# Last head of an expert-mixing attention layer: half of its output columns by slots instead of by dense products

## The chip, the cores and the metric

One core of one Trainium2 chip. The metric is the device time of the kernel in microseconds. TensorE (PE), VectorE (DVE), ScalarE (ACT), GpSimd (POOL) and SyncE (SP) run their own instruction streams side by side and wait for each other only through semaphores. SP issues most transfers; POOL issues the indirect ones.

## The reference, cut to what matters

`x` is 384 tokens by 1024. A graph attention layer is added to it first (the change does not touch it). Then comes a layer with 8 attention heads, each with 8 experts for its values and 8 experts for its output:

```python
gate_o = _get_sel_gate(x, sel_o_w, rs)        # per token and head: 8 gates, all but the best 2 are zero
ctx = jnp.einsum('bhqk,bhkp->bqhp', att, v)   # per token and head: 128 values
weighted = ctx[:, :, :, None, :] * gate_o[..., None]
out = jnp.einsum('bshep,hepd->bsd', weighted, o_w.reshape(H, E, P, D))
x = x + out
```

So a head's output is a sum over 8 experts, and for each token six of the eight terms are zero.

## The kernel before, in words

The kernel has two ways to compute a head's output.

**Dense.** All 8 experts for all tokens. The context is multiplied by each gate (`gate_context(e)` on DVE), turned on PE (`gated_turns(e)`), and split into a rounded part (`gc_hi_of`, ACT) and a rest (`gc_lo_of`, DVE). Weights come in units of 128 x 1024 through a ring of 3 buffers: SP loads (`load_unit`), ACT rounds (`hi_ring`), POOL or DVE makes the rest (`lo_of`). A product is three matmuls (`three`). One dense unit is 2 experts x 3 token tiles x 3 matmuls of 512 columns, for half of the output columns; 8 units (d0 to d7) cover the 1024 columns.

**By slots.** Each token with one of its two experts is a row, 768 rows a head. They are sorted by expert into 1024 slots, in lanes of 32 rows that share an expert. For head h: DVE scales the context rows (`gate_rows_of(h)`, 6 instructions); POOL scatters them to slots in DRAM (`scatter_rows`, 6 indirect transfers); SP loads the slots back (`load_slots`); PE turns them (`slot_turns`); ACT and DVE copy them out (`gcT_of`). DVE makes one-hot tables (`make_hots`), PE finds the output row of each slot from them (`rows_of_slots`), DVE stores it (`find_rows`). Then 8 rounds (`output_round(h, r)`) on PE, each 4 lanes x 2 column halves; of a round's four lanes two read their expert's weights where they were loaded, the other two a copy (`copy_out`, even ones on DVE, odd ones on ACT). After each round ACT and DVE bring the result from its banks to a stage (`y_out`), and POOL adds the stage's rows into `sums_scratch` in DRAM (`add_rows`, an indirect transfer that accumulates). The two rows of one token go to two different parts of `sums_scratch` (768 x 1024 in all), the first of which also holds x.

Heads 0 to 6 go by slots, head 7 is dense. The loop for h = 1 to 7 computes head h's queries, keys and values and attends, and in between does the slots of head h - 1. So in its last turn (h = 7) PE does the rounds of head 6: rounds 0 to 3, `f_attend(7)`, round 4, `context_turns(7)`, rounds 5 and 6, `gated_turns(0)`, round 7. After the loop the 8 dense units follow on PE.

The order on every engine is written out by hand. On POOL the loop's end is `lo_of` d0 and d1 and the eight `add_rows(6, i)`, then `lo_of` d3 to d7. `add_rows(h, 0)` waits until all eight adds of the head before have landed (`y_landed`), since an accumulating transfer must not meet another one on the same row. On SP, `load_sums` waits for all adds of head 6, then loads the two parts of the sums (3 tiles of 128 x 1024 each). DVE adds the parts (`add_sums`) and then the dense result of each column half (`add_out`, `add_out_tile`); SP stores six pieces of 128 x 512.

Of the kernel before, what the change touches and what calls it, by code (L numbers as in the profile page):

```python
# [14 lines left out]
P = 128  # L15
N = 384
NT = N // P
D = 1024
# [28 lines left out]
def ring_order():  # L47

    yield "v", 0, 0
    yield "router",  # L50
    yield "v", 0, 1
    for h in range(FH):
        yield "q", h
        yield "k", h
        for i in range(0 if h else 2, 8):
            yield "v", h, i
    for i in range(8):
        yield "d", i
# [36 lines left out]
OF_LAST = ((7, 5, 6), (0, 3, 4))  # L95
# [32 lines left out]
def landed(h):  # L128

    return 16 * h  # L130

# [33 lines left out]
def gnn_switch_kernel(nc, x_in, units, biases, bo, edge_type_weights, route_scale, edge_cols, src_row, dst_row, out):  # L165
# [5 lines left out]
    with ctx:  # L171
# [50 lines left out]
        gated = scratch[:, 4224:4992].rearrange("p (b n) -> p b n", b=2)  # L222
# [47 lines left out]
        row_of = edge_words[:, 0:(FH - 1) * SLOTS].rearrange("p (h i) -> p h i", h=FH - 1)  # L270
# [46 lines left out]
        gated_T, sums_landed, sums_added = sem("gated_T"), [sem(f"sums_landed{t}") for t in range(NT)], sem("sums_added")  # L317
        fq_hi_done, fq_lo_done, fk_hi_done, fk_lo_done = (sem("fq_hi_done"), sem("fq_lo_done"), sem("fk_hi_done"),
# [19 lines left out]
        def turned(g):  # L338
            return bank[(7, 6)[g]][:]
# [24 lines left out]
        def _(sp):  # L364
# [76 lines left out]
            for h in range(1, FH):  # L441
# [9 lines left out]
                load_unit(*(("q", h + 1) if h < FH - 1 else ("d", 0)))  # L451
                load_unit(*(("k", h + 1) if h < FH - 1 else ("d", 1)))
                load_unit(*(("v", h + 1, 0) if h < FH - 1 else ("d", 2)))
            def load_sums(n):
                if n == 0:
                    for b in range(STAGES):
                        sp.wait_ge(y_landed[b], landed(FH - 1))
                dst = x[:, n, :] if n < NT else y_rows[n - NT]
                sp.dma_start(dst, sums_dram[n * P:(n + 1) * P, :]).then_inc(sums_landed[n % NT], 16)
# [17 lines left out]
        def _(pool):  # L477
# [110 lines left out]

            lo_of("q", 0)
# [7 lines left out]
            for h in range(1, FH):  # L597
# [25 lines left out]
        def _(act):  # L623
# [209 lines left out]

            def q_hi(h):
# [5 lines left out]
            def gcT_of(h):  # L840
                act.wait_ge(slots_T, 2 * h + 1)
                act.activation(by_halves(gcT[:].rearrange("p a n -> p (a n)"), 0),
                               turned(0).rearrange("p (b n) -> p b n", n=GD), ACT.Copy).then_inc(gcT_act, 1)
# [29 lines left out]
            for h in range(1, FH):  # L873
# [19 lines left out]
                hi_ring(*(("q", h + 1) if h < FH - 1 else ("d", 0)))  # L893
                copy_out(h - 1, 9)
                hi_ring(*(("k", h + 1) if h < FH - 1 else ("d", 1)))
                hi_ring(*(("v", h + 1, 0) if h < FH - 1 else ("d", 2)))
# [14 lines left out]
            for e in range(1, FE):  # L911
                gc_hi_of(e)
                if e % 2:
                    if e > 1:
                        hi_ring("d", (e + 3) // 2)
            hi_ring("d", 6)
            hi_ring("d", 7)

# [3 lines left out]
        def _(dve):  # L922
# [524 lines left out]

            def gcT_of(h):
                dve.wait_ge(slots_T, 2 * h + 2)
                dve.tensor_copy(by_halves(gcT[:].rearrange("p a n -> p (a n)"), 1),  # L1450
                                turned(1).rearrange("p (b n) -> p b n", n=GD)).then_inc(gcT_dve, 1)
# [22 lines left out]

            def add_out(f, need, banks):
                dve.wait_ge(unit_used, need)
                for t in range(NT):
                    add_out_tile(f, t, banks)
# [59 lines left out]
            def gate_context(e):  # L1538
                if e == 0:
                    dve.wait_ge(context_T, FH)  # L1540
                    dve.wait_ge(gated_rows_landed, 16 * 6 * (FH - 1))
                if e >= 2:
                    dve.wait_ge(gated_T, e - 1)
                c = (GROUPS - 1) * FE + e
                dve.tensor_tensor(gated[:, e % 2, :].rearrange("p (t d) -> p t d", t=NT),
                                  bank[turned_bank(FH - 1)][:, 0:N].rearrange("p (t d) -> p t d", t=NT),
# [6 lines left out]
            def add_sums(t):  # L1553
                dve.wait_ge(sums_landed[t], 32)
                dve.tensor_tensor(x[:, t, :], x[:, t, :], y_rows[t], ALU.add).then_inc(sums_added, 1)

            gate_context(0)
            y_out(FH - 2, SLOTS - 3)
            gate_context(1)
            lo_of("d", 2)  # L1560
            y_out(FH - 2, SLOTS - 2)
            gc_lo_of(0)
            y_out(FH - 2, SLOTS - 1)
            gate_context(2)
            for e in range(1, FE):
                gc_lo_of(e)
                if e + 2 < FE:
                    gate_context(e + 2)
            for t in range(NT):
                add_sums(t)  # L1570
# [508 lines left out]
```

## Time and profile before

| what | value |
|---|---|
| median of 3 runs | 824.06 us (823.68 to 826.8) |
| profiled execution, its own time | 826.44 us |
| its span, first to last instruction | 824.4 us |
| granted TensorE clock over the span | 0.998 |
| busy: PE, DVE, POOL, ACT | 812.7, 489.0, 461.0, 376.4 us |

The span is what the trace shows. The profiled execution's own time is 2.04 us more than its span, and 2.38 us more than the median. Times in rows below are microseconds from the span's start; a matmul's duration overlaps the next one, so its pace is read from the starts.

### The profile page before, as it was taken

The numbers are of one execution on the slowest core, as the hardware profiler recorded it, in microseconds if no ns is written. First come the engines' busy times: TensorE is split into PE (matmuls) and PEld (weight loads), VectorE is DVE, ScalarE is ACT, GpSimd is POOL, SyncE is SP. The second block draws the span as 40 slices with busy tenths as digits, with TensorE's granted clock in tenths as the row PEclk, the third lists the DMA queues.
The fourth block names the chain that finished last, engine by engine and source line by source line (L and its number), as shares of the span: only waits on it lengthen the run. The fifth ranks groups of instructions, "written<-read, shape, count | busy, mean of one in ns | idle before, by whom it ended". The sixth has DMA issues, their size and how long they took to land.

```text
span 824.4 us, 14155 instructions
## 1 busy us (share of the span) xinstructions
PE 812.7 (99%) x5016; PEld 650.6 (79%) x5016; DVE 489.0 (59%) x1112; ACT 376.4 (46%) x615; POOL 461.0 (56%) x296
## 2 busy tenths in 40 slices
PE   8999999999999999999999999999999999999998
PEld 7999998888888778898578578578578588588476
DVE  7999973444444155998554554655655545645645
ACT  5333335555665343334624634634634534535531
POOL 4577875343334434547664665565674665664652
PEclk9999999999999999999999999999999999999999
DMA  8666663442222328643598597597597597697684
GB/s 295 185 194 178 201 191 107 144 136 81 97 76 78 103 77 323 213 129 134 122 245 304 119 266 273 125 264 269 132 271 258 131 264 261 140 257 262 147 217 172
DMA packets 66177, 153.38 MB, mean 186 GB/s; under 512 B 9392, under 2 KB 22320, under 8 KB 66128
## 3 DMA queue, kind: packets, MB, share of 16 engines
q1 hardware_dynamic: 51472, 120.73, 42.7%
q0 software_dynamic: 10944, 24.82, 16.5%
q10 hardware_dynamic: 3712, 7.18, 3.2%
q8 instruction: 30, 0.49, 0.3%
q14 instruction: 19, 0.16, 0.1%
HBM read 122.06 MB, written 37.97 MB: 194 GB/s over the span
## 4 chain that ended last, share of the span: by engine, by line
PE 83%; POOL 4%; issue 4%; DMA 3%; DVE 3%; ACT 1%; SPq 0%; ACTq 0%; DVEq 0%; POOLq 0%
PE bank L1586 22%; PE bank L1588 21%; PE bank L1587 21%; PE bank L1917 12%; POOL mask_scratch L501 3%; PE bank L1640 2%; PE bank L1729 2%; PE bank L1633 2%; PE bank L1701 2%; DVE scratch L1004 1%; DMA w_raw<-in_units 1%; DMA mask_scratch<-scratch,cell 1%; POOL w_lo L497 1%; DMA mask<-mask_scratch 0%; ACT scratch L725 0%
## 5 line engine op out<-in xcount | busy, mean ns | idle before, releaser
L557 POOL TENSOR_TENSOR w_lo<-w_raw,w_hi 128x1024 fp32r<-128x1024 f32 x67 | 164.4, 2456 | 140.3 <-ACT w_hi L812 132.2
L1586 PE MATMUL bank<-w_hi,hT_hi 128*128 128x512 f32 x480 | 190.1, 396 | 1.9 <-POOL w_lo L548 1.2
L1588 PE MATMUL bank<-w_hi,hT_lo 128*128 128x512 f32 x480 | 187.5, 391 | 0.0
L1587 PE MATMUL bank<-w_lo,hT_hi 128*128 128x512 f32 x480 | 187.5, 391 | 0.0
L497 POOL TENSOR_TENSOR w_lo<-w_raw,w_hi 128x1024 fp32r<-128x1024 f32 x39 | 94.7, 2431 | 103.7 <-ACT w_hi L640 83.5
L812 ACT ACTIVATE w_hi<-w_raw 128x1024 fp32r<-128x1024 f32 x84 | 88.7, 1056 | 127.0 <-PE bank L1588 98.9
L1586 PE MATMUL bank<-hT_hi,w_hi 128*128 128x384 f32 x320 | 108.2, 338 | 1.2 <-POOL w_lo L497 1.2
L1586 PEld LDWEIGHTS bank<-w_hi,hT_hi 128*128 128x128 f32 x480 | 90.6, 189 | 21.7 <-POOL w_lo L548 1.7
L1588 PE MATMUL bank<-hT_hi,w_lo 128*128 128x384 f32 x320 | 107.1, 335 | 0.0
L1587 PE MATMUL bank<-hT_lo,w_hi 128*128 128x384 f32 x320 | 107.1, 335 | 0.0
L1588 PEld LDWEIGHTS bank<-w_hi,hT_lo 128*128 128x128 f32 x480 | 90.1, 188 | 19.1
L1587 PEld LDWEIGHTS bank<-w_lo,hT_hi 128*128 128x128 f32 x480 | 90.2, 188 | 17.4
L1917 PE MATMUL bank<-late,gcT 128*32 128x512 f32 (+1 forms) x868 | 100.6, 595 | 0.0
L1917 PEld LDWEIGHTS bank<-late,gcT 128*32 128x32 f32 x868 | 26.7, 109 | 57.2 <-issue 55.0
L501 POOL DMA_INDIRECT mask_scratch<-scratch,cell x48 | 56.9, 1185 | 23.8 <-issue 12.9
L1586 PE MATMUL bank<-large,w_hi 128*128 128x384 f32 x192 | 66.5, 346 | 0.0
L1586 PEld LDWEIGHTS bank<-hT_hi,w_hi 128*128 128x128 f32 x320 | 60.2, 188 | 7.3 <-issue 5.0
L1587 PE MATMUL bank<-large,w_hi 128*128 128x384 f32 x192 | 65.0, 339 | 0.0
L1588 PE MATMUL bank<-large,w_lo 128*128 128x384 f32 x192 | 64.9, 338 | 0.0
L1414 DVE COPY late<-late 128x1024 f32 x56 | 60.6, 1112 | 6.3 <-issue 5.3
L1587 PEld LDWEIGHTS bank<-hT_lo,w_hi 128*128 128x128 f32 x320 | 60.1, 188 | 0.0
L1588 PEld LDWEIGHTS bank<-hT_hi,w_lo 128*128 128x128 f32 x320 | 60.1, 188 | 0.0
(228 smaller groups left out, 1279.6 us busy)
## 6 DMA issues: line engine op xcount, KB each, us to landing
w_raw<-in_units SPq DMA_DIRECT2D x145, 512.0 KB, 3.9
late<-in_units SPq DMA_DIRECT2D x56, 512.0 KB, 7.7
scratch<-slots_scratch SPq DMA_DIRECT2D x7, 512.0 KB, 7.3
scratch<-in_src_row ACTq DMA_DIRECT2D x8, 384.0 KB, 4.3
scratch<-in_dst_row ACTq DMA_DIRECT2D x8, 384.0 KB, 6.3
sums_scratch<-zeros SPq DMA_DIRECT2D x1, 1536.0 KB, 8.3
sums_scratch<-x SPq DMA_DIRECT2D x1, 1536.0 KB, 11.3
x<-sums_scratch SPq DMA_DIRECT2D x3, 512.0 KB, 4.8
```

What stands on the lines that cost most here:

```text
L497: pool.tensor_tensor(w_lo[:, s, :], w_raw[:, s, :], w_hi[:, s, :].bitcast(fp32), ALU.subtract).then_inc(lo_ready[s], 1)
L501: pool.indirect_dma_start(out=mask_dram, out_offset=bass.IndirectOffsetOnAxis(ap=cells, axis=0), in_=values, in_offset=None, bounds_check= ...
L557: pool.tensor_tensor(w_lo[:, s, :], w_raw[:, s, :], w_hi[:, s, :].bitcast(fp32), ALU.subtract).then_inc(lo_ready[s], 1)
L812: act.activation(w_hi[:, s, :], w_raw[:, s, :], ACT.Copy).then_inc(hi_ready, 1)
L1414: dve.tensor_copy(copied[:, m % COPY_BUFS, :], late[:, bass.ds(copy_value[m // 2], D)]).then_inc(copied_dve, 1)
L1586: pe.matmul(dst, a_hi, b_hi, start=first, stop=False)
L1587: pe.matmul(dst, a_hi, b_lo, start=False, stop=False)
L1588: return pe.matmul(dst, a_lo, b_hi, start=False, stop=last)
L1633: return pe.transpose(dst, src, ident[:])
L1640: last = pe.transpose(banks[g][:, i * GD:(i + 1) * GD], block[rows, :], ident[rows, rows])
L1701: last = pe.matmul(bank[NT * head + t][:, 0:N], a[p, tok], b[p, :], start=n == 0, stop=n == 2)
L1917: last = pe.matmul(bank[YF[r % 2][f]][lane * LANE:(lane + 1) * LANE, :], gcT[:, r // 4, c:c + LANE], weights, start=True, stop=True)
```

## The change

Head 7's output columns 512 to 1023 stay dense (units d4 to d7, now the only ones in the ring). Its columns 0 to 511 go by slots, in eight half rounds (`last_round`) with one bank each. Their weights (units d0 to d3) are loaded straight to `o_raw`. For head 7 there are now also `gate_rows_of`, six `scatter_rows` (put between `add_rows(6, 3)` and `add_rows(6, 4)`), `load_slots`, `slot_turns`, `make_hots`, `rows_of_slots`, `find_last_rows`, 15 copies of 512 columns, eight `last_y_out` and eight `last_add_rows`, whose rows are 512 wide. The sums are loaded in two lots: columns 512 to 1023 once head 6's adds have landed, columns 0 to 511 once head 7's have. Round 3 of head 6 is moved behind `f_attend(7)`, round 4 behind `context_turns(7)`, and ACT's `context_of(7)` ahead of `y_out(6, 3)`. Whole for SP and POOL; for the others the orders are written on fewer lines:

```diff
-OF_LAST = ((7, 5, 6), (0, 3, 4))
+OF_LAST = (7, 3, 4)
+LAST = FH - 1
...
-gated = scratch[:, 4224:4992].rearrange("p (b n) -> p b n", b=2)
+gated = [copied[:, b, HALF:HALF + N] for b in (8, 9)]
...
 # sync: after the loads of the last turn (d4, d5, d6)
-for i in range(3, 7):
-    load_unit("d", i)
-for n in range(NT):
-    load_sums(n)
 load_unit("d", 7)
-for n in range(NT, 2 * NT):
-    load_sums(n)
-for f in range(2):
-    for t in range(NT):
-        sp.wait_ge(out_added, 2 * NT + NT * f + t + 1)
-        sp.dma_start(out_tiles[:, t, f * HALF:(f + 1) * HALF],
-                     x[:, t, f * HALF:(f + 1) * HALF]).then_inc(out_stored, 16)
+sp.wait_ge(y_done, SLOTS * LAST)
+for i in range(4):
+    sp.dma_start(out_part(o_raw, 2 * i),
+                 units[PLACE["d", i]].rearrange("p (k n) -> p k n", k=2)).then_inc(o_landed, 16)
+load_slots(LAST)
+def load_sums(f, landings):
+    cols = slice(f * HALF, (f + 1) * HALF)
+    for n in range(2 * NT):
+        t = n % NT
+        dst = x[:, t, :] if n < NT else stage(t)
+        sp.dma_start(dst[:, cols], sums_dram[n * P:(n + 1) * P, cols]).then_inc(landings[t], 16)
+for b in range(STAGES):
+    sp.wait_ge(y_landed[b], landed(LAST))
+load_sums(1, sums_landed)
+for b in range(STAGES):
+    sp.wait_ge(y_landed[b], landed(FH))
+load_sums(0, last_landed)
+for t in range(NT):
+    sp.wait_ge(out_added, 2 * NT + t + 1)
+    sp.dma_start(out_tiles[:, t, HALF:D], x[:, t, HALF:D]).then_inc(out_stored, 16)
...
 # gpsimd
+def last_add_rows(i):
+    if i % 2:
+        pool.wait_ge(y_dve, last_dve_rows(i + 1))
+    else:
+        pool.wait_ge(y_act, last_act_rows(i + 1))
+    if i == 0:
+        pool.wait_ge(rows_known, FH)
+        for b in range(STAGES):
+            pool.wait_ge(y_landed[b], landed(LAST))
+    pool.indirect_dma_start(out=sums_dram.rearrange("r (f n) -> (r f) n", f=2),
+                            out_offset=bass.IndirectOffsetOnAxis(ap=row_of[:, LAST, i:i + 1], axis=0),
+                            in_=stage(i)[:, 0:HALF], in_offset=None, bounds_check=4 * N - 1,
+                            oob_is_err=False, compute_op=ALU.add).then_inc(y_landed[i], 16)
...
-        lo_of("d", 0)
-        lo_of("d", 1)
+        lo_of("d", 4)
+        lo_of("d", 5)
     for i in range(SLOTS):
+        if h == LAST and i == 4:
+            for k in range(2):
+                for t in range(NT):
+                    scatter_rows(LAST, k, t)
         add_rows(h - 1, i)
-for i in range(3, 8):
-    lo_of("d", i)
+lo_of("d", 7)
+for i in range(SLOTS):
+    last_add_rows(i)
...
 # scalar (last_copy_out and last_y_out: as on vector)
+            if h == LAST and i == 3:
+                context_of(h)
             y_out(h - 1, i, 0)
-            if i == 3:
+            if h < LAST and i == 3:
                 context_of(h)
...
+gc_hi_of(1), (2), (3); hi_ring("d", 7); copy_experts(LAST)
+last_copy_out(1), (3); gc_hi_of(4); gcT_of(LAST); gc_hi_of(5); last_copy_out(5), (7)
+last_y_out(0); last_copy_out(9); last_y_out(2); last_copy_out(11); last_y_out(4)
+last_copy_out(13); last_y_out(6); gc_hi_of(6), (7)
+for t in range(NT):
+    act.wait_ge(last_added, t + 1)
+    act.dma_start(out_tiles[:, t, 0:HALF], x[:, t, 0:HALF]).then_inc(out_stored, 16)
...
 # vector
+def last_copy_out(m):
+    if m == 0:
+        dve.wait_ge(o_landed, 16 * (8 * LAST + 4))
+        dve.wait_ge(y_done, SLOTS * LAST)
+    if m >= COPY_BUFS:
+        dve.wait_ge(y_done, SLOTS * LAST + (m - COPY_BUFS) // 2 + 1)
+    dve.tensor_copy(copied[:, m % COPY_BUFS, 0:HALF],
+                    late[:, bass.ds(copy_value[m // 2], HALF)]).then_inc(copied_dve, 1)
+def last_y_out(i):
+    dve.wait_ge(y_done, SLOTS * LAST + i + 1)
+    dve.wait_ge(y_landed[i], landed(LAST))
+    dve.tensor_copy(stage(i)[:, 0:HALF], bank[5 + i % 2][:]).then_inc(y_dve, 1)
+def add_sums(t, f, landings, done):
+    cols = slice(f * HALF, (f + 1) * HALF)
+    dve.wait_ge(landings[t], 32)
+    dve.tensor_tensor(x[:, t, cols], x[:, t, cols], stage(t)[:, cols], ALU.add).then_inc(done, 1)
...
 # order after y_out(6, 3), copy_out 12, y_out(6, 4), copy_out 14 (h - 1 = 6 as before)
+gate_rows_of(LAST); y_out(6, 5); gate_context(0); y_out(6, 6); gate_context(1)
+lo_of("d", 6); gc_lo_of(0); y_out(6, 7); gate_context(2); make_hots(LAST)
+gc_lo_of(1); gate_context(3); gc_lo_of(2); gate_context(4); gc_lo_of(3); gate_context(5)
+find_last_rows(); copy_experts(LAST); last_copy_out(0), (2); gc_lo_of(4); gate_context(6)
+gcT_of(LAST); last_copy_out(4), (6); gc_lo_of(5); gate_context(7); last_copy_out(8)
+last_y_out(1); last_copy_out(10); last_y_out(3); last_copy_out(12); last_y_out(5)
+last_copy_out(14); last_y_out(7); gc_lo_of(6), (7)
+add_sums(t, 1, ...) for t in 0, 1, 2; add_out_tile for t in 0, 1, 2 (as each tile's products end)
+add_sums(t, 0, last_landed, last_added) for t in 0, 1, 2
...
 # tensor
-        for r in range(4):
+        early = 3 if h == LAST else 4
+        for r in range(early):
             output_round(h - 1, r)
         f_attend(h)
-        output_round(h - 1, 4)
+        output_round(h - 1, early)
         context_turns(h)
-        for r in range(5, SLOTS):
+        for r in range(early + 1, SLOTS):
             output_round(h - 1, r)
...
+def last_round(r):
+    n = SLOTS * LAST + r
+    if r == 0:
+        pe.wait_ge(gcT_act, FH)
+        pe.wait_ge(gcT_dve, FH)
+        pe.wait_ge(o_landed, 16 * (8 * LAST + 4))
+    if r >= 2:
+        if r % 2:
+            pe.wait_ge(y_dve, last_dve_rows(r - 1))
+        else:
+            pe.wait_ge(y_act, last_act_rows(r - 1))
+    pe.wait_ge(copied_dve, dve_copies(LAST, r))
+    pe.wait_ge(copied_act, act_copies(LAST, r))
+    for lane in range(4):
...
+            last = pe.matmul(bank[5 + r % 2][lane * LANE:(lane + 1) * LANE, :],
+                             gcT[:, r // 4, c:c + LANE], weights, start=True, stop=True)
+    last.then_inc(y_done, 1)
 gated_turns(1)
-for n in range(7):
-    dense_unit(n)
+dense_half(0, 0); dense_half(0, 1)      # each: 9 matmuls, then gated_turns(k + 2)
+rows_of_slots(LAST)
+dense_half(1, 0); dense_half(1, 1)
+pe.wait_ge(slots_landed, 16 * FH)
+pe.wait_ge(rows_known, FH)
+slot_turns(LAST)
+dense_half(2, 0)
+direct_experts(LAST)
+for r in range(SLOTS):
+    last_round(r)
+dense_half(2, 1)
 s = unit_ready(0, R["d", 7])
+pe.wait_ge(gc_lo_done, FE)
```

Waits on the ring units and the unchanged rest of `dense_half` (as `dense_unit`, with t = 1 of the first waiting for all `y_out` of head 6) are left out above. `find_last_rows` is `find_rows` with row numbers doubled.

## Rows read from the trace of the kernel before

**Rows 1.** The page: busy time by engine; chain that ended last, by line.
```profile
PE 812.7 (99%) x5016; PEld 650.6 (79%) x5016; DVE 489.0 (59%) x1112; ACT 376.4 (46%) x615; POOL 461.0 (56%) x296
...
PE bank L1586 22%; PE bank L1588 21%; PE bank L1587 21%; PE bank L1917 12%; POOL mask_scratch L501 3%; PE bank L1640 2%; PE bank L1729 2%; PE bank L1633 2%; PE bank L1701 2%; DVE scratch L1004 1%; DMA w_raw<-in_units 1%; DMA mask_scratch<-scratch,cell 1%; POOL w_lo L497 1%; DMA mask<-mask_scratch 0%; ACT scratch L725 0%
```

**Rows 2.** The chain in order of time, 740 to 826: start, length, what.
```profile
768.87 7.00 PE bank L1917 x64
...
777.66 1.85 PE bank L1917 x16
...
785.89 0.48 PE bank L1633 x3
...
788.43 0.33 PE bank L1633 x3
...
821.26 0.69 DVE x L1472
```

**Rows 3.** Timeline of PE: start, length, instruction.
```profile
759.62 0.71 PE L1640 MATMUL bank<-ident,scratch 64*128 64x64 f32 x16
...
802.02 0.39 PE L1586 MATMUL bank<-w_hi,hT_hi 128*128 128x512 f32 x1
802.70 0.39 PE L1586 MATMUL bank<-w_hi,hT_hi 128*128 128x512 f32 x1
```

**Rows 4.** Timeline of DVE: start, length, instruction.
```profile
719.59 1.64 DVE L1468 TENSOR_SCALAR scratch<-bank,scratch 128x128 f32<-128x128 f32 x6
...
756.14 0.95 DVE L1433 TENSOR_TENSOR mask<-mask,scratch 128x768 bf16<-128x768 f32 x1
...
774.12 0.54 DVE L1062 TENSOR_TENSOR v_lo<-scratch,v_hi 128x384 fp32r<-128x384 f32 x1
...
775.94 0.69 DVE L1459 COPY x<-bank 128x512 f32<-128x512 f32 x1 [1.27 <-PE bank L1917]
...
807.11 6.98 DVE L1555 TENSOR_TENSOR x<-x,scratch 128x1024 f32<-128x1024 f32 x3 [5.20 <-DMA scratch<-sums_scratch]
```

**Rows 5.** Timeline of POOL: start, length, instruction.
```profile
728.20 1.02 POOL L569 DMA_INDIRECT slots_scratch<-scratch,cell  x1 [0.30 <-issue]
...
734.88 1.30 POOL L569 DMA_INDIRECT slots_scratch<-scratch,cell  x1 [0.30 <-issue]
...
772.64 1.64 POOL L585 DMA_INDIRECT sums_scratch<-scratch,edge  x1 [4.10 <-ACT scratch L853]
...
785.92 1.54 POOL L585 DMA_INDIRECT sums_scratch<-y_more,edge  x1 [0.30 <-issue]
787.77 1.54 POOL L585 DMA_INDIRECT sums_scratch<-y_more,edge  x1 [0.30 <-issue]
```

**Rows 6.** The add of line 585 issued at 776.47: time to landing, all columns equal.
```profile
DMA to landing us min/median/max: 7.7/7.7/7.7
```

**Rows 7.** All 56 adds of line 585: time to landing.
```profile
DMA to landing us min/median/max: 6.2/8.9/12.8
```

**Rows 8.** All 42 scatters of line 569: time to landing.
```profile
DMA to landing us min/median/max: 2.2/6.1/7.9
```

**Rows 9.** DMA issues, 740 to 826: line, count, KB each, median us to landing.
```profile
x<-sums_scratch SPq DMA_DIRECT2D x3, 512.0 KB, 4.8
scratch<-sums_scratch SPq DMA_DIRECT2D x3, 512.0 KB, 7.3
out_x<-x SPq DMA_DIRECT2D x6, 256.0 KB, 2.1
scratch<-slots_scratch SPq DMA_DIRECT2D x1, 512.0 KB, 7.4
...
sums_scratch<-y_more,edge POOLq DMA_INDIRECT x2, 9.9
```

**Rows 10.** Timeline of SP's queue.
```profile
798.09 1.28 SPq L459 DMA_DIRECT2D x<-sums_scratch  x3
```

**Rows 11.** Stretch 802 to 804: busy time by engine, PE clock, DMA share, GB/s.
```profile
802.00:804.00 2.00, 2.00 (x10) 1.66 (x9) 0.00 (x0) 0.26 (x1) 1.66 (x1) 1.00 1.02 408
```

More of the change, by code:

```diff
@@ L56, in ring_order @@
             yield "v", h, i
-    for i in range(8):
+    for i in range(4, 8):
         yield "d", i
@@ L450, in _ @@
                     load_out(h - 1, 7)
[L451 to L459, printed above, removed]
@@ L909, in _ @@
                         gc_hi_of(0)
[L911 to L916, printed above, removed]
-            hi_ring("d", 7)
+            gc_hi_of(1)
+            gc_hi_of(2)
+            gc_hi_of(3)
+            hi_ring("d", 7)
+            copy_experts(LAST)
+            last_copy_out(1)
+            last_copy_out(3)
+            gc_hi_of(4)
+            gcT_of(LAST)
+            gc_hi_of(5)
+            last_copy_out(5)
+            last_copy_out(7)
+            last_y_out(0)
+            last_copy_out(9)
+            last_y_out(2)
+            last_copy_out(11)
+            last_y_out(4)
+            last_copy_out(13)
+            last_y_out(6)
+            gc_hi_of(6)
+            gc_hi_of(7)
+            for t in range(NT):
+                act.wait_ge(last_added, t + 1)
+                act.dma_start(out_tiles[:, t, 0:HALF], x[:, t, 0:HALF]).then_inc(out_stored, 16)
         @block.vector
@@ L1446, in find_rows, with find_last_rows @@
                                   ALU.add).then_inc(rows_known, 1)
+            def find_last_rows():
+                dve.wait_ge(rows_found, FH)
+                step.add(dve.tensor_scalar(in_tile[:, 0, :], bank[5][:, SLOTS:2 * SLOTS], 2.0 * P, 2048.0, ALU.mult,
+                                           ALU.add))
+                settled()
+                dve.scalar_tensor_tensor(row_of[:, LAST, :], bank[5][:, 0:SLOTS], 2.0, in_tile[:, 0, :], ALU.mult,
+                                         ALU.add).then_inc(rows_known, 1)
             def gcT_of(h):
@@ L1557, in _ @@
+            gate_rows_of(LAST)
+            y_out(LAST - 1, SLOTS - 3)
             gate_context(0)
-            y_out(FH - 2, SLOTS - 3)
+            y_out(LAST - 1, SLOTS - 2)
             gate_context(1)
-            lo_of("d", 2)
-            y_out(FH - 2, SLOTS - 2)
+            lo_of("d", 6)
             gc_lo_of(0)
-            y_out(FH - 2, SLOTS - 1)
+            y_out(LAST - 1, SLOTS - 1)
             gate_context(2)
-            for e in range(1, FE):
+            make_hots(LAST)
+            for e in range(1, 4):
@@ L1566, in _ @@
                 gc_lo_of(e)
-                if e + 2 < FE:
-                    gate_context(e + 2)
+                gate_context(e + 2)
+            find_last_rows()
+            copy_experts(LAST)
+            last_copy_out(0)
+            last_copy_out(2)
+            gc_lo_of(4)
+            gate_context(6)
+            gcT_of(LAST)
+            last_copy_out(4)
+            last_copy_out(6)
+            gc_lo_of(5)
+            gate_context(7)
+            last_copy_out(8)
+            for i in range(1, SLOTS, 2):
+                last_y_out(i)
+                if i < SLOTS - 1:
+                    last_copy_out(9 + i)
@@ L1577, in _ @@
                     dve.wait_ge(unit_used, R["d", 7] + 1)
-                add_out_tile(1, t, OF_LAST[1])
+                add_out_tile(1, t, OF_LAST)
+            for t in range(NT):
+                add_sums(t, 0, last_landed, last_added)
         @block.tensor
@@ L1871, in slot_turns @@
             def slot_turns(h):
-                turn_by_halves((turned(0), turned(1)), [slots[:, n, :] for n in range(SLOTS)], slots_T)
+                turn_by_halves((turned(h, 0), turned(h, 1)), [slots[:, n, :] for n in range(SLOTS)], slots_T)
             def rows_of_slots(h):
@@ L1925, in gated_turns @@
                 for t in range(NT):
-                    last = turn(bank[1 + e % 2][:, t * P:(t + 1) * P], gated[:, e % 2, t * P:(t + 1) * P])
+                    last = turn(bank[1 + e % 2][:, t * P:(t + 1) * P], gated[e % 2][:, t * P:(t + 1) * P])
                 last.then_inc(gated_T, 1)
@@ L2007, in _, with dense_half @@
-            gated_turns(1)
-            for n in range(7):
-                dense_unit(n)
+            def dense_half(i, kk):
+                s = R["d", 4 + i] % RING
+                k = 2 * i + kk
+                c = slice(kk * HALF, (kk + 1) * HALF)
+                pe.wait_ge(gc_lo_done, k + 1)
+                for t in range(NT):
+                    if k == 0 and t == 1:
+                        pe.wait_ge(y_act, act_rows(SLOTS * LAST))
+                        pe.wait_ge(y_dve, dve_rows(SLOTS * LAST))
+                    tok = slice(t * P, (t + 1) * P)
+                    last = three(bank[OF_LAST[t]][:, 0:HALF], hT_hi[:, k, :][:, tok], hT_lo[:, k, :][:, tok],
+                                 w_hi[:, s, c], w_lo[:, s, c], k == 0, False)
+                if kk:
+                    last.then_inc(unit_used, 1)
+                if k + 2 < FE:
+                    gated_turns(k + 2)
@@ L2014, in _ @@
                     c = slice(kk * HALF, (kk + 1) * HALF)
[L2015 removed]
+                    last = three(bank[OF_LAST[t]][:, 0:HALF], hT_hi[:, 6 + kk, :][:, tok], hT_lo[:, 6 + kk, :][:, tok],
                                  w_hi[:, s, c], w_lo[:, s, c], False, kk == 1)
```

91 lines of the change are left out of this document (48 added, 43 removed).

## The prediction

> **What bounds the kernel now.** I read the page's busy times first: TensorE is busy 99% of the span, the next engine 59% [rows 1]. The chain by lines puts over 80% of the span on TensorE lines (22, 21, 21 and 12% are the largest, [rows 1]). In order of time, from 768.87 to 821 the chain does not leave TensorE: rounds of head 6, then dense products, then one last add on VectorE at 821.26 [rows 2]. So before the change an instruction less on TensorE in that stretch is time less. Sums, loads and adds all have slack: the accumulated sums were asked for at 798.09 and added from 807.11 [rows 10, 4], 14 us before the end. The change trades TensorE work for a longer string of transfers, so I follow both.
>
> **TensorE's work, step by step.** Starts of every third dense matmul are 0.68 us apart [rows 3], so 0.227 us each. Four units of 18 go: 72 x 0.227 = 16.3 us. Added: a full round of head 6 takes 1.75 us (four in 7.00, [rows 2]), a half round 0.875, eight 7.0 us; the slot turns 0.7 (16 of them in 0.71, [rows 3]); the six small matmuls of `rows_of_slots` at most as much, I take 0.3. Net 16.3 - 8.0 = 8.3 us less. If all else were hidden, the span would be 824.4 - 8.3 = 816.1. It is not, for these reasons.
>
> **Until the gated rows are ready.** Rounds 0 to 2 of head 6 end at 768.87 + 5.25 = 774.1. `f_attend(7)` now stands next and needs v_lo, which ends at 774.66 [rows 4]; it takes 1.8 us (775.87 to 777.66, [rows 2]), to 776.5. Round 3 goes to 778.3, context turns (0.48, [rows 2]) to 778.8, round 4 (1.85) to 780.6. The moved round makes the context ready a round earlier, but VectorE has `y_out(6, 4)` ahead of `gate_rows_of(7)` in its order, and round 4 now stands behind the turns, so the gain is lost again: `y_out` 0.69 [rows 4] to 781.4, copy 14 as much, to 782.0, the six gated rows 1.64 [rows 4] to 783.65. Behind them VectorE still has `y_out(6, 5)` and `gate_context(0)` (0.55, as v_lo of the same width), so `gated_turns(0)` can start at 784.9 and round 7 ends at about 787.2, where it ended at 785.89 before [rows 2]: 1.4 us lost. `gate_context(1)`, the rest of d6 and `gc_lo_of(0)` hold the first dense product to 787.9.
>
> **POOL's queue.** The six scatters wait at its head for the gated rows; behind them queue `add_rows(6, 4)` to `(6, 7)`, and behind these the rest of d7 and all of head 7's adds. Scatters start every 1.34 us (five steps from 728.20 to 734.88, [rows 5]): first 783.9, last 790.6, queue free at 792.2. Adds start every 1.85 us (785.92, 787.77, [rows 5]): add 7 starts at 797.75, ten us later than before. Landing takes 6.2 us at least, 8.9 in the middle, 12.8 at most [rows 7]; the one at 776.47, third in its row, took 7.7 [rows 6], and since the first four adds of head 6 are long done here I take that: all of head 6 has landed at 805.4.
>
> **The slots.** The last scatter lands 6.1 us after its issue [rows 8]: 796.7. The load of the slots took 7.4 us behind other loads, a load of the same size against little else 4.8 [rows 9]; here four adds are under way beside it and I take the middle, 6.1: 802.8. TensorE arrives earlier: 787.9, four dense steps with turns of 2.4 us each (nine matmuls 2.04, turns 0.33 from [rows 2]) make 797.5, `make_hots` on VectorE (0.95 for its longest instruction [rows 4], some 1.5 in all) delays `gc_lo_of(1)` by 0.8, `rows_of_slots` 0.3: 798.6. It idles 4.2 us. The loads of `o_raw`, asked for at 787.3, land under the dense steps. Then slot turns to 803.5, a dense step to 805.9 (it covers the copies to gcT), the first half round to 806.8, `last_y_out(0)` to 807.6. Seven more rounds end at 812.9; a round may wait up to a full 1.85 us each time before POOL, which comes next, would notice. TensorE goes on: dense step to 815.3, 1.2 us for the last context split with nothing left to cover it, the last unit (4.1) to 820.6, an add and a store behind it. Its own end would be at 823.7: of 8.3 us only 0.7 are left, even if the sums cost nothing.
>
> **The sums.** `last_add_rows(0)` needs both its stage (807.6) and all adds of head 6 (805.4). Eight adds at 1.85 us: the last starts at 807.6 + 7 x 1.85 = 820.6. The trace has no add of rows of 512 columns. The issue is bounded by a scatter's 1.34 below and 1.85 above, and I take 1.85, the same kind of instruction; the landing lies between 2.1 (a plain transfer of 256 KB, [rows 9]) and 7.7, and I take 6.2, the fastest add [rows 7], as POOL feeds the engines slower than they work at half width. Last landing 826.8. Now what was hidden is bare: SP issues six loads 0.43 us apart (three in 1.28, [rows 10]); the pair for tile 0 is complete with the fourth. Four of 256 KB at 408 GB/s [rows 11] are 2.6 us, with the start some 4.1; the bounds are 3.4 (fourth issue and 2.1) and 7.3 [rows 9]. VectorE adds three tiles of 512 columns, half of 6.98 us [rows 4]: 3.5. From the end of its last add to the end of the span stands 824.4 - 821.95 = 2.45 us (an issue and the 2.1 of a store). Sum: 826.8 + 4.1 + 3.5 + 2.45 = 836.9.
>
> One rule of the Trainium skill speaks for a shorter tail. DMA: Bandwidth & Descriptors, in its section on the anatomy of a GpSimd-issued transfer, fits each one by 2.0 us plus its bytes over 436 GB/s; by that an add of 256 KB would land in 2.6 us and the sum would be 833.3. The trace does not agree for adds: by the same fit a full one would take 3.2 us, and none took under 6.2 [rows 7].
>
> Against its own execution the change adds 836.9 - 824.4 = 12.5 us. The profiled execution took 826.44, 2.04 over its span and 2.38 above the median of 824.06. I take the difference to the median: 824.06 + 12.5 = 836.6.
>
> **The rivals.**
> *Cheap half rows.* An add of half width costs POOL what a scatter costs, and lands as a plain transfer of its size. For it: scatters of short rows issue faster [rows 5]. Against it: the scatter is not shorter only in bytes, it also does not accumulate. Gain 7 x 0.51 = 3.6 and 6.2 - 2.1 = 4.1, so 828.9. Chance 0.20.
> *Crowded transfers.* The slots load takes 7.4 (+1.3), the last add 7.7 (+1.5), the sums 7.3 (+3.2): 842.6. For it: such times stand in the rows of this stretch. Against it: they were taken beside ring loads, which have ended by then. Chance 0.15.
> *The sums come home under the dense products* (the other side). TensorE sets the end, as before. It decides if the last add lands before 823.7 - 10.05 = 813.6, ten us being loads, adds and store. From 805.4 that leaves eight adds 8.2 us, landing included; that needs an issue of 0.8 us, which no indirect transfer shows. The span is then 823.7, and 819.5 if the slots are back before TensorE asks: 823.4 or 819.2 against the median. Chance 0.10, half of it on each side of the line below.
> *The change does not save TensorE work*: half rounds that cost as much as full ones (7 us more) would end TensorE at 830.7, under the sums, and change nothing of the forecast. No chance of its own.
> The forecast keeps 0.55, with 832 to 841 as its own range (slots load, landing and sums each by a part of their bounds).
>
> **How the numbers follow.** Under 0.5%, that is 4.1 us, I count as no change, which is what a measurement of this kernel can tell. Faster (under 819.9): 0.05. Same: 0.05 of the last rival and 0.03 from the low end of cheap half rows, 0.08. Slower: 0.87. The range takes in most of cheap half rows and nearly all of crowded transfers: 828.5 to 842.
>
> **What the changed profile would show.** The chain of its last 40 us leaves TensorE: POOL's indirect adds one after another, then a wait for the last landing, sums loads, three adds on VectorE, a store. TensorE stands idle about 4 us before the slot turns, and ends some 16 us before the span does. The scatters of head 7 start near 784, `add_rows(6, 7)` near 798, the first half-width add near 807, the last near 820. The forecast is wrong if half-width adds start under 1.4 us apart, if they land in under 4 us, or if the last product of TensorE is still followed within 4 us by the end.

## The result, and the profile after

The changed kernel takes 846.78 us (median of 4 runs, 844.63 to 848.35), the one before 824.2 us. The ratio is 1.0273 (95% interval 1.0259 to 1.0287): slower by 22.6 us. The direction was forecast, the size was not: 836.6 us with a range up to 842.0.

The profiled execution took 845.3 us in its span. What stands ahead of the change took 3 us less than in the profile of before, and this part varies from one execution to the next. So below, times are also counted from one mark, the start of round 0 of head 6 (768.80 before, 765.71 after). From the mark to the end of the span it is 55.6 us before and 79.6 after. TensorE's last product begins 52.0 us after the mark before (820.83) and 61.4 after (827.14). Mark and last product, in the kernel before and then in the changed one:

```profile
768.80 7.07 PE L1917 MATMUL bank<-late,gcT 128*32 x64
...
820.83 0.39 PE L1588 MATMUL bank<-w_hi,hT_lo 128*128 128x512 f32 x1
```
```profile
765.71 5.36 PE L2020 MATMUL bank<-late,gcT 128*32 x48
...
827.14 0.39 PE L1691 MATMUL bank<-w_hi,hT_lo 128*128 128x512 f32 x1
```

The chain that ended last, in order of time (start, length, what), for the changed kernel; it answers to [rows 2]:

```profile
788.84 5.03 DMA slots_scratch<-scratch,cell
793.89 12.14 DMA scratch<-slots_scratch
806.07 1.12 PE bank L1743 x16
...
824.77 1.54 POOL sums_scratch L615
...
826.61 5.05 DMA sums_scratch<-y_more,edge
...
833.06 6.64 DMA scratch<-sums_scratch
839.72 1.95 DVE x L1638 x3
```

Before, this stretch was TensorE only. Now it is transfers: a scatter, the slots' way back, the half-width adds, the sums' way back. The two longest pieces are loads, and both took longer than I gave them.

POOL's timeline of the changed kernel, against [rows 5]:

```profile
776.90 1.54 POOL L602 DMA_INDIRECT sums_scratch<-x,edge  x1 [1.98 <-DVE x L1535]
781.35 1.01 POOL L586 DMA_INDIRECT slots_scratch<-scratch,cell  x1 [2.91 <-DVE scratch L1544]
...
788.84 0.97 POOL L586 DMA_INDIRECT slots_scratch<-scratch,cell  x1 [0.30 <-issue]
790.11 1.57 POOL L602 DMA_INDIRECT sums_scratch<-x,edge  x1 [0.30 <-issue]
...
795.81 1.55 POOL L602 DMA_INDIRECT sums_scratch<-y_more,edge  x1 [0.30 <-issue]
...
813.62 1.55 POOL L615 DMA_INDIRECT sums_scratch<-scratch,edge  x1 [13.89 <-ACT scratch L882]
...
826.61 1.56 POOL L615 DMA_INDIRECT sums_scratch<-y_more,edge  x1 [0.30 <-issue]
```

The first half-width add waited 13.89 us for its stage, which ACT had filled at 812.87:

```profile
812.27 0.60 ACT L882 ACTIVATE scratch<-bank 128x512 f32<-128x512 f32 x1 [3.03 <-PE bank L2130]
```

Eight of them took 12.99 us from first to last start, 1.86 each: at half the width an add costs POOL what a full one does.

Stretches of the changed kernel: busy time of PE, PEld, DVE, ACT, POOL, then TensorE's granted clock, DMA share, GB/s.

```profile
792.00:794.00 2.00, 2.00 (x12) 1.65 (x10) 0.34 (x1) 0.36 (x1) 1.70 (x2) 1.00 1.10 243
...
796.00:798.00 2.00, 0.00 (x0) 0.00 (x0) 0.23 (x1) 0.00 (x0) 2.00 (x2) 1.00 1.00 181
...
800.00:802.00 2.00, 0.00 (x0) 0.00 (x0) 0.00 (x0) 0.00 (x0) 0.00 (x0) 0.50 0.57 122
...
808.00:810.00 2.00, 2.00 (x6) 1.52 (x6) 1.88 (x5) 1.23 (x3) 0.00 (x0) 0.50 0.83 267
```

TensorE stands idle from 795 to 806, its granted clock falls from 1.00 to 0.50 (2.4 to 1.2 GHz), and the dense products behind the slot turns still run at 0.50: they start every 0.43 us (the x6 of the last line), where they started every 0.23 us before the wait (the x12 of the first line counts three short turns too).

### The profile page after: what moved, and what is told of

Same layout as the page of the kernel before. It is cut to its first block, busy times and chain, and to the rows that moved or that the text cites. A ratio compares the mean times of both kernels' runs of the same rounds, so it can differ in the third digit from the quotient of the medians.

```text
span 845.3 us, 14299 instructions
## 1 busy us (share of the span) xinstructions
PE 805.0 (95%) x5028; PEld 638.8 (76%) x5028; DVE 496.6 (59%) x1137; ACT 378.3 (45%) x623; POOL 468.9 (55%) x306
## 4 chain that ended last, share of the span: by engine, by line
PE 85%; DMA 4%; DVE 4%; POOL 2%; issue 2%; ACT 1%; ACTq 0%; POOLq 0%; SPq 0%; DVEq 0%
PE bank L1689 23%; PE bank L1691 22%; PE bank L1690 22%; PE bank L2020 10%; PE bank L1743 3%; PE bank L1832 2%; PE bank L1804 1%; DMA scratch<-slots_scratch 1%; PE bank L1736 1%; DMA scratch<-sums_scratch 1%; PE bank L2130 1%; POOL mask_scratch L518 1%; DMA sums_scratch<-y_more,edge 1%; DMA slots_scratch<-scratch,cell 1%; DMA x<-in_x 1%
## 5 line engine op out<-in xcount | busy, mean ns | idle before, releaser
L574 POOL TENSOR_TENSOR w_lo<-w_raw,w_hi 128x1024 fp32r<-128x1024 f32 x63 | 157.0, 2495 | 127.4 <-ACT w_hi L848 119.2
L1689 PE MATMUL bank<-w_hi,hT_hi 128*128 128x512 f32 x456 | 181.6, 398 | 3.3 <-DVE hT_lo L1130 1.4
L1690 PE MATMUL bank<-w_lo,hT_hi 128*128 128x512 f32 x456 | 178.7, 392 | 0.0
L1691 PE MATMUL bank<-w_hi,hT_lo 128*128 128x512 f32 x456 | 178.7, 392 | 0.0
L514 POOL TENSOR_TENSOR w_lo<-w_raw,w_hi 128x1024 fp32r<-128x1024 f32 x39 | 95.0, 2438 | 101.5 <-ACT w_hi L676 81.8
L848 ACT ACTIVATE w_hi<-w_raw 128x1024 fp32r<-128x1024 f32 x80 | 84.5, 1056 | 122.1 <-PE bank L1691 87.8
L1689 PEld LDWEIGHTS bank<-w_hi,hT_hi 128*128 128x128 f32 x456 | 86.5, 190 | 23.7 <-issue 3.8
L1691 PEld LDWEIGHTS bank<-w_hi,hT_lo 128*128 128x128 f32 x456 | 86.0, 189 | 18.2
L1690 PEld LDWEIGHTS bank<-w_lo,hT_hi 128*128 128x128 f32 x456 | 86.2, 189 | 16.5
L518 POOL DMA_INDIRECT mask_scratch<-scratch,cell x48 | 54.1, 1128 | 25.6 <-issue 12.2
L1691 PE MATMUL bank<-large,w_lo 128*128 128x384 f32 x192 | 64.3, 335 | 0.0
L1690 PE MATMUL bank<-large,w_hi 128*128 128x384 f32 x192 | 64.3, 335 | 0.0
L586 POOL DMA_INDIRECT slots_scratch<-scratch,cell x48 | 52.0, 1083 | 17.0 <-issue 13.7
## 6 DMA issues: line engine op xcount, KB each, us to landing
sums_scratch<-x SPq DMA_DIRECT2D x1, 1536.0 KB, 11.2
```

Source lines behind the costliest of these rows:

```text
L514: pool.tensor_tensor(w_lo[:, s, :], w_raw[:, s, :], w_hi[:, s, :].bitcast(fp32), ALU.subtract).then_inc(lo_ready[s], 1)
L518: pool.indirect_dma_start(out=mask_dram, out_offset=bass.IndirectOffsetOnAxis(ap=cells, axis=0), in_=values, in_offset=None, bounds_check= ...
L574: pool.tensor_tensor(w_lo[:, s, :], w_raw[:, s, :], w_hi[:, s, :].bitcast(fp32), ALU.subtract).then_inc(lo_ready[s], 1)
L586: pool.indirect_dma_start(out=slots_dram, out_offset=bass.IndirectOffsetOnAxis(ap=slot_of[:, c:c + 1], axis=0), in_=gated_rows[:, k, t, :] ...
L848: act.activation(w_hi[:, s, :], w_raw[:, s, :], ACT.Copy).then_inc(hi_ready, 1)
L1689: pe.matmul(dst, a_hi, b_hi, start=first, stop=False)
```

## The experiments

All are edits of the changed kernel unless said. An idle matmul is one whose result nobody reads; it only keeps TensorE busy. "Held" adds are adds of head 6 that POOL issues only once head 7's slots are back. "From the mark" is from round 0 of head 6 to the end of the span, in the profiled execution of each.

| run | time, us | ratio to before (95%) | from the mark |
|---|---|---|---|
| before | 824.2 | | 55.6 |
| changed | 846.78 | 1.0273 (1.0259 to 1.0287) | 79.6 |
| adds held | 848.07 | 1.0292 (1.0276 to 1.0307) | 77.7 |
| two adds held | 845.32 (one run) | | 76.9 |
| stores first | 844.22 | 1.0231 (1.0199 to 1.0262) | 78.9 |
| 36 idle matmuls | 844.63 | 1.024 (1.0225 to 1.0256) | 77.8 |
| 46 idle matmuls | 845.02 | 1.0258 (1.0241 to 1.0275) | 76.4 |
| no adds of head 7 | 835.69 | 1.0127 (1.0077 to 1.0177) | 66.5 |
| the same, held and kept busy | 832.96 | 1.0108 (1.0091 to 1.0125) | 63.5 |
| mended | 843.85 | 1.0241 (1.0224 to 1.0258) | 76.7 |
| mended, POOL's rest of d7 early | 845.41 | 1.0265 (1.0248 to 1.0282) | 76.4 |
| no chain | 831.09 | 1.0084 (1.0067 to 1.01) | 64.3 |
| no chain, no adds 4 to 7 | 822.45 | 0.9984 (0.9975 to 0.9994) | 54.4 |
| before, moved round alone | 824.96 | 1.0008 (0.9999 to 1.0017) | 56.3 |

### Why the slots came so late

```diff
                 for t in range(NT):
                     scatter_rows(LAST, k, t)
+            pool.wait_ge(slots_landed, 16 * FH)
         add_rows(h - 1, i)
```

> The changed kernel, with POOL waiting for the slots of head 7 to be back before it issues the adds of head 6 from round 4 on. Theory A: the slots load took 12.1 us because it shares the DMA engines with these four adds and lands only when they do. Then it lands in 4 to 5.5 us here, TensorE's idle time before the slot turns falls from 11 us to under 5, but the four adds start about 9 us later and head 7's first add still starts at 812 to 816, so the time is 843 to 849 us. Theory B: pieces of 512 bytes are slow by themselves. Then the load still takes 10 us or more, the adds start 16 us later and the time is over 853 us.

The load of the slots landed in 4.0 us (the first line is its landing; then TensorE's first slot turn, and POOL's last add of head 6 with the first of head 7):

```profile
DMA to landing us min/median/max: 4.0/4.0/4.0
```
```profile
798.77 0.71 PE L1744 MATMUL bank<-ident,scratch 64*128 64x64 f32 x16 [2.92 <-DMA scratch<-slots_scratch]
```
```profile
805.21 1.55 POOL L602 DMA_INDIRECT sums_scratch<-y_more,edge  x1 [0.30 <-issue]
...
814.11 1.55 POOL L615 DMA_INDIRECT sums_scratch<-scratch,edge  x1 [4.94 <-DMA sums_scratch<-y_more,edge]
```

Theory A holds for the load: alone it takes a third of 12.1 us. But the time did not move. The four adds now start 9 us later and land at 813.3, and `last_add_rows(0)` waits for them instead of for the rounds (the note on its idle time names them). It starts 47.5 us after the mark, in the changed kernel 47.9: one wait was changed into another of nearly the same length.

Two adds held (`i == 6`):

> The changed kernel with only the last two adds of head 6 held until the slots are back (four held: the slots load landed in 4.0 us; none held: 12.1 us). Theory A: the load takes turns with the adds on the engines, so it lands about when the two that are under way do: 7 to 9 us. Theory B: it waits for whatever is queued when it is issued and is then fast: as both adds are issued before it, they land in 8 us and it in 8 + 4: 11 us or more.

The load landed in 6.7 us, between 4.0 and 12.1, at 801.4; the two adds beside it landed at 797.5 and 800.0. A little faster than I gave it, and far from theory B. So the load's time grows with the adds that run beside it: 4.0, 6.7, 12.1 us with none, two, four. (With four it took 12.1 us in the profile of the changed kernel and 10.6 to 11.2 in those of four later runs with the same four adds beside it: no adds of head 7, the stores first, 36 and 46 idle matmuls.) The Trainium skill says in DMA: Bandwidth & Descriptors, in its section on queues, rings and completion order, that each DMA engine takes turns between its queues and drains a whole packet, a group of pieces, at each turn. By that, if the packets of both hold about as many pieces, a load in pieces of 512 bytes moves few bytes for each turn that it gives to an add with rows of 4 KB. The three times go that way; no run varied the size of the pieces. I had treated landing of adds and load as two separate numbers (805.4 and 802.8), and they are one.

### What the clock cost

```diff
+            pe.wait_ge(rows_known, FH)
+            for _ in range(36):
+                pe.matmul(bank[6][:, 0:HALF], hT_hi[:, 0, 0:P],
+                          w_hi[:, R["d", 5] % RING, 0:HALF], start=True, stop=True)
             pe.wait_ge(slots_landed, 16 * FH)
-            pe.wait_ge(rows_known, FH)
```

> The changed kernel, with 36 matmuls of 512 columns, whose result nobody reads, in TensorE's wait for the slots. Theory A: the granted clock fell to 0.50 in that wait, and slot turns and dense products behind it ran at 0.43 us a matmul in place of 0.23. Then the clock stays at 1.00, the first add of head 7 starts 2 to 2.6 us earlier and the time is 844 to 845 us. Theory B: something else sets the first add: under 0.7 us gained.

The time, 844.63 us, lies in the range of theory A, but not by its mechanism: from the first slot turn to the first half round it took 4.8 us (5.06 in the changed kernel). The matmuls ended at 804.3, TensorE was idle for 2 us, and its clock fell after that. The first half-width add still came 1.2 us earlier from the mark, for another reason: the slots load landed in 10.9 us instead of 12.1. With 46:

> As the one with 36 matmuls that nobody reads, but with 46, since with 36 TensorE was idle for 2 us before the slots landed and the clock fell all the same (0.71 and 0.50 in the next 4 us). Theory A: kept busy up to the slots it keeps its clock of 1.00, and the rounds start 3.1 us after the slot turns began instead of 5.06; from round 0 of head 6 to the end 77.7 us instead of 79.6, the time 844 to 845.5 us. Theory B: the clock is not on the path: 79 us or more, 846 us or more.

The same two stretches, 36 matmuls first, then 46 (columns as above):

```profile
806.00:808.00 2.00, 1.67 (x18) 1.41 (x19) 0.83 (x2) 0.86 (x2) 0.00 (x0) 0.71 0.09 14
808.00:810.00 2.00, 2.00 (x6) 1.56 (x5) 1.79 (x5) 1.15 (x3) 0.00 (x0) 0.50 0.87 295
```
```profile
806.00:808.00 2.00, 2.00 (x23) 1.45 (x22) 0.70 (x2) 0.74 (x2) 0.00 (x0) 1.00 0.06 18
808.00:810.00 2.00, 2.00 (x14) 1.44 (x16) 1.92 (x5) 1.28 (x3) 0.00 (x0) 1.00 0.99 295
```

The rounds begin 3.25 us after the slot turns instead of 5.06, as expected: the lower clock cost 1.8 us on the path. From the mark to the end it took 3.2 us less than the changed kernel, more than the clock gave: the slots load took 10.9 us here as well. The time, 845.02, is 1.8 us under the changed kernel's, but the intervals of the ratios overlap, so the gain is shown by the trace and only hinted at by the times.

### What the sums cost

> The changed kernel without the eight adds of head 7 (its columns 0 to 511 are computed and staged, but never added to the sums). Theory A: two causes lie one behind the other, TensorE's wait and the tail of the sums. Then TensorE ends as in the changed kernel (828.3 in the span), the rest follows in 4 to 6 us, and the time is 834 to 836 us, still 10 us over the kernel before. Theory B: the tail is all: the time is 822 to 826 us.

835.69 us: about half of the 22.6 us lies behind the adds of head 7 (11.1 in the medians), and without them the kernel is still 11.4 us slower than before. These halves are rough, as the four runs went from 829.84 to 838.94. In the profile the last product begins at 827.79, which is 60.0 us after the mark, where it was 52.0 before, and the end comes 66.5 us after it instead of 55.6. So 8.0 of these 10.9 us are TensorE's own delay, and the rest is the longer end behind its last product. DVE's end in that kernel:

```profile
828.22 0.69 DVE L1546 TENSOR_TENSOR x<-bank,x 128x512 f32<-128x512 f32 x1 [0.67 <-PE bank L1689]
828.82 1.89 DVE L1636 TENSOR_TENSOR x<-x,scratch 128x512 f32<-128x512 f32 x3
```

The stores of columns 512 to 1023, moved ahead of the second load of the sums on SP:

> The changed kernel, with the three stores of columns 512 to 1023 ahead of the second load of the sums in SP's queue. Theory A: in the changed kernel they run beside that load and slow it (its last pieces took 6.8 us). Then these land in about 5 us and the time is 844 to 845.5 us. Theory B: the load of rows of 2 KB is slow alone: no change, 846.5 to 847.

Inconclusive in time: 844.22, its runs from 840.73 to 846.92, its interval overlapping that of the changed kernel. In the trace both theories are half right. The last pieces of the sums landed in 5.5 us instead of 6.8, as A says. But the stores now ran beside the last adds, and the last of these landed in 7.1 us instead of 5.0. And even alone the six loads took 6.6 us from the first issue to the first sum on DVE, where I had 4.1: between 834 and 840 they moved 188 to 354 GB/s and about 255 in the mean of the six stretches of 1 us, not the 408 that I had read beside loads of 4 KB rows. The length of the rows alone does not explain it: in slices of 0.25 us the same six loads went from 385 GB/s (near 835.3) down to 131 (near 836.8) and up to 369 again. What slowed them in between is open.

### Is TensorE's saving real?

> As the last one without head 7's adds, and besides head 6's adds from round 4 on wait for the slots, and 12 matmuls that nobody reads fill TensorE's wait. Theory A: with the slots load alone on the engines and the clock kept, TensorE ends 8 to 9 us earlier, at about 820 in the span, and the time is 825 to 829 us: even without the adds and with the wait mended no gain is left on the kernel before. Rival: y_out of rounds 4 to 7 now waits for the held adds to land and the rounds stall instead: TensorE ends at 824 or later, the time is over 830 us.

832.96 us, where the rival's time lies, but not by its mechanism. TensorE's last product begins at 819.57, as theory A has it: 53.0 us after the mark, 1.0 later than before the change. The slots were there in 4.0 us and the slot turns began at 798.89. Then the rounds stood still for 1.80 us, behind a copy of 512 columns on DVE that took 2.89 us; others took 0.42. The rows are TensorE's, DVE's and POOL's of that kernel:

```profile
809.78 1.99 PE L2129 MATMUL bank<-late,gcT 128*32 x14 [1.80 <-DVE late L1626]
```
```profile
806.70 2.89 DVE L1626 COPY late<-late 128x512 f32 x1
```
```profile
806.34 2.96 POOL L574 TENSOR_TENSOR w_lo<-w_raw,w_hi 128x1024 fp32r<-128x1024 f32 x1
```

The copy ends 0.3 us after POOL's instruction does (809.6 and 809.3). And both loads of the sums waited for the held adds, to 813.7, once more a wait changed into another one, so the end came 10.5 us after TensorE's last product began.

> The changed kernel without head 7's six scatters and eight adds, and with its slots loaded without waiting for them (columns 0 to 511 of head 7 are computed from old slots and not added). Theory A: the saving on TensorE is real and is lost to the chain of transfers alone: 50 to 52 us from round 0 of head 6 to the end, the time 818.5 to 821 us, faster than the kernel before. Rival: copies, y_out and the changed order eat it as well: 823 us or more.

831.09 us lies in the rival's range, but neither theory holds. With no scatter to wait for, the slots load was issued at 788.71, right behind 2 MB of weights and amid the last adds of head 6, and took 14.2 us: the same contention at another place, so this run did not isolate what it should. The next one left those adds out too:

> In the last kernel without a chain the slots load met head 6's adds and the weight loads and took 14.2 us. So here head 6's adds of rounds 4 to 7 are left out too, beside head 7's scatters and adds, and its slots are loaded without waiting; the sums are incomplete. Theory A: with slots there in time TensorE ends 48 us after round 0 of head 6 begins (52.4 in the kernel before), 4 of the 8.3 us that its removed products are worth; the rest goes to waits of the new order (gate rows, one-hot tables, last context split). The end follows 6 us later, as stores of columns 0 to 511 come last: 54 us, and 822 to 823.5 us in all. Theory B: all of the 8.3 us show up: under 820 us. Theory C: TensorE still ends at 52 or later, over 826 us: the half rounds themselves are dear.

822.45 us, ratio 0.9984 (0.9975 to 0.9994): theory A. Its last product begins 48.8 us after the mark, 3.2 less than before. TensorE's rows of this kernel show where the other 5 us of 8.3 went:

```profile
772.32 0.44 PE L1685 MATMUL bank<-pT_hi,v_hi 128*128 128x384 f32 x1 [0.56 <-DVE v_lo L1126]
...
782.38 0.55 PE L1732 MATMUL bank<-ident,late 128*128 128x128 f32 x3 [0.59 <-DVE late L1609]
...
799.16 5.83 PE L2126 MATMUL bank<-late,gcT 128*32 x48
805.35 1.98 PE L2126 MATMUL bank<-late,gcT 128*32 x14 [0.36 <-ACT late L872]
...
811.20 0.47 PE L1685 MATMUL bank<-w_hi,hT_hi 128*128 128x512 f32 x1 [1.26 <-DVE hT_lo L1126]
```

Waits of 0.56 (v_lo), 0.59 (gated context), 0.36 (a copy), 1.26 (last split), and half rounds of 0.97 us (six in 5.83) for my 0.875: 8 x 0.1 = 0.8. That makes 3.6. The slots load, which took 8.5 us beside the weight loads alone (14.2 with the adds as well), cost 0.25, and the context split that stands behind the one-hot tables 0.16; the rest is spread over small gaps. So even with the whole chain cut out, which the computation does not allow, the change would be worth 0.2% (0.06 to 0.25).

The moved round by itself, in the kernel before:

> The kernel before, with only the moved round (round 3 of head 6 behind f_attend(7), round 4 behind the context turns, the context copy ahead of y_out 3). Theory of the prediction: the attention waits 0.5 us for v_lo, nothing is gained: 824.4 to 825.2 us. Rival: the earlier context helps gate_context(0) and the dense products start sooner: under 823.8 us.

824.96 us, ratio 1.0008 (0.9999 to 1.0017), 0.65 us more from the mark. The attention waits 0.56 us for v_lo, as the prediction said, and nothing comes back. The size fits the wait, but the interval still takes in no change at all.

### All mended

```diff
-            if h == LAST and i == 4:
+            if h == LAST and i == 5:
...
+                pool.wait_ge(slots_landed, 16 * FH)
```

with 12 idle matmuls and the stores first.

> The changed kernel with all that the runs so far suggest: head 6's fourth add ahead of the scatters, its last three held until the slots are back, 12 matmuls that nobody reads in TensorE's wait, the stores of columns 512 to 1023 ahead of the second load of the sums. Theory A: the path is POOL's adds one after another, so only an add moved ahead (1.9 us) and the stores (1.4 us) count: 74 to 75 us from round 0 of head 6 to the end, the time 842 to 844 us, still 2% over the kernel before. Rival: TensorE's stalls are the path: mended they give 8 us, under 839 us.

843.85 us. The time is in theory A's range; the 76.7 us from the mark are 2 more than it gave, since the stores slowed the last adds again (6.9 us for the last one). TensorE was hardly idle before the slots, and it did not matter: the first half-width add began at 812.19, 0.9 us after head 6's last add had landed (803.52 and 7.8 us). No version that computes the whole result beats the kernel before.

The copy beside POOL came up here as well (3.00 us). The last run makes POOL's rest of d7 earlier, while POOL waits for the slots, and puts the stores back:

> The mended kernel without its stores first, and with POOL's rest of d7 (lo_of) made before the slots are awaited instead of behind the held adds. In the three kernels with held adds a copy of 512 columns on VectorE took 3.0 to 3.3 us instead of 0.42, and it ran while POOL made that rest, and TensorE's rounds stood still for 1.6 to 1.9 us behind it. Theory A: the copy waits for POOL's instruction, as both use the same way into the memory. Then all these copies take 0.4 to 0.5 us here and the rounds run without a gap over 0.5 us; the time stays at 842.5 to 845 us, since the first half-width add waits for the held adds to land, not for the rounds. Theory B: the copy waits for something of the new order: it still takes 3 us.

DVE's and TensorE's rows in it:

```profile
804.75 0.53 DVE L1628 COPY late<-late 128x512 f32 x1
...
806.70 0.42 DVE L1628 COPY late<-late 128x512 f32 x1
```
```profile
808.35 2.00 PE L2131 MATMUL bank<-late,gcT 128*32 x14 [0.36 <-ACT late L877]
```

Theory A, in the trace: the longest of its six copies took 0.62 us, and no gap between the rounds was over 0.36. In the four kernels where a copy met POOL's rest of d7 (adds held, two adds held, no adds held and kept busy, mended) it took 2.89 to 3.46 us and ended 0.3 us after POOL's instruction. The Trainium skill says in SBUF — State Buffer, in its section on who interferes with whom, that a VectorE copy, where it runs in a mode with two ports, and a GpSimd instruction take one shared pair of ports in turn, each for the whole instruction; the rows agree. The time, 845.41 us, is 0.4 us over the range that I gave. No gain was expected of it: the half-width adds began at 811.95, behind the held adds. TensorE's last product begins 51.5 us after the mark here, 0.5 less than in the kernel before, though some 3 us of waiting for the slots, filled by the 12 idle matmuls, are still in it.

## Why the prediction was right and wrong

**Right: the sign and the outline of the mechanism.** The sum had the end set by scatter, slots load, eight adds, their landing, the sums' load and a store, and that is the chain that the trace shows. TensorE's own waits eat its saving (0.7 us are left in the prediction, with the slots 4.2 us late; 0.5 in the last run, with them some 3 us late), and the last adds go one by one on POOL: their starts span 12.99 us for my 12.95.

**Right: up to the scatters.** Counted from the mark, the gated rows were due at 783.65 - 768.8 = 14.85 us; the last of them ended at 14.9 (780.57 in the changed kernel). The last scatter was issued after 23.1 us (I had 21.8) and landed in 5.0 instead of 6.1.

**Wrong: "the slots load", the term of 6.1 us.** It took 12.1, that is 6 us more, since the four adds of head 6 ran beside it. The two ends that I had, 4.8 and 7.4 [rows 9], were a load of wide rows and the slots' load of head 6 behind plain loads. The seven slots' loads of the kernel before took 4.0 to 7.9 us, and none of them had an add beside it, so the range should have been left open above for that. The runs with four and with two adds held show the cause (4.0 and 6.7 us).

**Wrong with it: nothing for the clock.** I let TensorE idle for 4 us and then run at full pace. It idled 11, and ran at 0.50 behind it: 1.8 us by the run with 46 matmuls. With the 0.7 us between stage and POOL's issue, and the scatters' 1.3 more and 1.1 less from above, that is 8.7 of the 9.1 us by which the first half-width add was late: it came 47.9 us after the mark, where I had 38.8.

**Wrong: "the sums", the term of 4.1 us.** It was 8.0 (831.75 to 839.72). By the run with the stores first some 1.4 of it are the stores beside it; the rest is the rate, 255 GB/s there where I took 408 from a stretch of 4 KB rows. Why the rate was lower stays open.

```profile
831.75 1.27 SPq L479 DMA_DIRECT2D x<-sums_scratch  x3
```

**Smaller terms.** The landing of the last add was 5.05 for my 6.2, DVE's three sums 1.95 for 3.5, the last store 3.6 for 2.45.

In all: 9.1 (first add late) - 1.1 + 3.9 - 1.6 + 1.2 = 11.5 us over my sum, counted from the mark, where the sum gave 68.1 and the trace 79.6. The Trainium skill's rule of 2.0 us and the bytes over 436 GB/s (DMA: Bandwidth & Descriptors, anatomy of a GpSimd-issued transfer), which the prediction set aside, is not met by half-width adds either: 4.7 to 5.6 us where it gives 2.6.

The crowded rival came nearest, but its 842.6 was still 4 us short. It had too small a price on the slots load (7.4 for 12.1) and on the sums (7.3 for 8.0), it named ring loads and not adds as the neighbours of the slots load, and its crowded last add (7.7) did not come (5.05). None of the prediction's own signs of being wrong came up: the half-width adds started 1.86 us apart, landed in over 4 us, and the end followed TensorE's last product by 18 us. All three guarded against too short a tail, none against too long a one. One reading was loose: the 14 us of slack for the sums before run to the last add; to the end of the span they are 17.3.

## What to carry to other kernels

Work taken off the busiest engine at the end of a kernel is only saved if what replaces it does not lengthen the string of transfers behind it; count that string with every landing in it before counting instructions. Where a load in small pieces ran beside accumulating transfers of wide rows, it landed 0.2 to 1.4 us after the last of them (four and two adds): give them one common landing time, not one each. And where two chains of nearly equal length meet in one instruction, mending one of them shows nothing in the time.

## What the runs showed of the hardware

An indirect add took POOL 1.54 to 1.57 us and started every 1.86 us with rows of 2 KB; with rows of 4 KB it took 1.54 to 1.64 us for the last eight, and two in a row started 1.87 to 1.95 us apart. Five of the six last scatters, which do not accumulate, took 0.97 to 1.01. In the changed kernel half-width adds landed in 4.7 to 5.6 us (up to 8.0 in the runs with held adds), the last four full ones in 6.6 to 10.0. A load of 512 KB in pieces of 512 bytes landed in 4.0 us with nothing beside it, 6.7 with two adds, 10.6 to 12.1 with four, and 14.2 beside adds and four weight loads. TensorE's clock was still 1.00 while it idled its last 2 us before the slots in the run with 36 matmuls, and fell to 0.50 only once it was working again, where it stayed until about 810. A VectorE copy of 512 columns, 0.42 us by itself, took 2.9 to 3.5 us when it met POOL's 128 x 1024 instruction (2.95 to 2.97 us).
